# An LSTM ahead of a six-layer transformer: input projection kept in float32, its bf16 parts made later

## The reference, cut to what matters

```python
xW = jnp.einsum('ntd,dk->tnk', x, Wx) + b          # 1024 steps, 2 rows, 4*256 columns
def step(carry, xw_t):
    prev_h, prev_c = carry
    a = xw_t + prev_h @ Wh
    i, f, o = sigmoid(a[:, :H]), sigmoid(a[:, H:2*H]), sigmoid(a[:, 2*H:3*H])
    g = tanh(a[:, 3*H:])
    next_c = f * prev_c + i * g
    next_h = o * tanh(next_c)
    return ((next_h, next_c), next_h)
_, hs = jax.lax.scan(step, (h0, c0), xW)
# then, six times: attn_layer (windows of 64 keys) and ffn_layer, all in float32
```

## Time and profile before

| | |
|---|---|
| median of 3 runs | 5177.27 us (5176.47 to 5178.69) |
| profiled execution: span | 5175.6 us |
| profiled execution: own time | none is recorded; the median is 1.7 us above the span |
| busy over the span | PE 92%, PEld 72%, DVE 67%, ACT 50%, POOL 37% |
| LSTM stage (prologue and 136 steps) | until about 600 us |
| mean granted clock of PE | 0.934 of 2.4 GHz |

### The profile page before, as it was taken

How to read it: one execution, slowest core, us unless ns; L and a number is a source line. 1 busy time by engine, 2 the same in 40 slices (tenths; PEclk the granted TensorE clock), 3 DMA queues, 4 the chain that set the end, 5 groups by cost and what they waited for, 6 DMA issues and landing times.

```text
span 5175.6 us, 192189 instructions
## 1 busy us (share of the span) xinstructions
PE 4769.9 (92%) x79632; PEld 3728.4 (72%) x79632; DVE 3483.0 (67%) x14167; ACT 2608.7 (50%) x8192; POOL 1913.4 (37%) x2070
## 2 busy tenths in 40 slices
PE   4665699999999999999999999999999999999887
PEld 1445487777777787777777787777777787776666
DVE  8665577676676677677676677676676677676554
ACT  0112255555555555555555555555555555555654
POOL 3650233333333333333333333333333333334442
PEclk6555699999999999999999999999999999999999
DMA  3020122322322422322322422322322422323341
GB/s 131 2 88 0 38 83 81 117 86 88 114 83 80 124 82 81 117 85 87 113 84 81 123 82 81 116 86 84 117 84 80 122 83 81 117 85 106 109 130 48
DMA packets 311365, 463.54 MB, mean 90 GB/s; under 512 B 213264, under 2 KB 239888, under 8 KB 297616
## 3 DMA queue, kind: packets, MB, share of 16 engines
q1 hardware_dynamic: 310544, 451.92, 28.8%
HBM read 381.93 MB, written 69.93 MB: 87 GB/s over the span
## 4 chain that ended last, share of the span: by engine, by line
PE 63%; DVE 11%; issue 7%; POOL 4%; ACT 3%; POOLq 0%; DVEq 0%; ACTq 0%
PE mm L908 14%; PE gates L185 12%; PE st L1020 8%; PE gates L177 5%; PE dd L1020 4%; PE st L947 3%; PE pt L1047 3%; PE tt L920 3%; PE pt L1055 3%; PE pt L961 3%; DVE qk L1342 2%; POOL va L811 2%; DVE pr L1392 2%; PE dd L977 2%; PE st L989 1%
## 5 line engine op out<-in xcount | busy, mean ns | idle before, releaser
L796 POOL TENSOR_TENSOR turned<-raw,rotl 128x256 f32<-128x256 f32 x768 | 712.6, 943 | 1667.1 <-ACT raw L1139 1356.7
L908 PE MATMUL mm<-wqkv,xa 128*128 128x512 f32 x2304 | 1166.3, 618 | 12.3 <-DVE xa L1305 8.4
L185 PE MATMUL gates<-hp,whp 128*128 128x6 bf16 x28672 | 849.2, 165 | 22.1 <-DVE hp L230 22.1
L185 PEld LDWEIGHTS gates<-hp,whp 128*128 128x128 bf16 x28672 | 784.3, 96 | 56.8 <-DVE hp L230 29.4
L1190 ACT ACTIVATE pr<-st,nb,qn 128x128 f32<-128x128 f32 x1536 | 688.5, 464 | 36.7 <-DVE nb L1380 36.2
L192 ACT ACTIVATE state<-gsum 128x16 f32<-128x16 f32 x896 | 195.4, 218 | 1009.9 <-DVE gsum L200 1003.6
L908 PEld LDWEIGHTS mm<-wqkv,xa 128*128 128x128 f32 x2304 | 384.2, 193 | 241.6 <-issue 222.8
L200 DVE TENSOR_REDUCE gsum<-gates 128x16 f32<-128x48 f32 x896 | 183.1, 204 | 526.1 <-PE gates L185 526.1
L177 PEld LDWEIGHTS gates<-hp,whp 128*128 128x128 bf16 x14336 | 423.2, 96 | 141.5 <-issue 85.6
L177 PE MATMUL gates<-hp,whp 128*128 128x2 bf16 x14336 | 485.8, 163 | 26.2 <-DVE hp L215 26.2
L804 POOL TENSOR_TENSOR qn<-ss,power 128x8 f32<-128x8 f32 x192 | 320.6, 1670 | 496.7 <-DVE ss L1351 487.5
(11 more groups left out here) (135 smaller groups left out, 9778.8 us busy)
## 6 DMA issues: line engine op xcount, KB each, us to landing
wqkv<-in_Wqkv SPq DMA_DIRECT2D x288, 512.0 KB, 4.4
w<-in_W SPq DMA_DIRECT2D x48, 1364.0 KB, 6.1
wo<-in_Wo SPq DMA_DIRECT2D x48, 1024.0 KB, 4.9
w<-in_W SPq DMA_DIRECT2D x48, 768.0 KB, 4.5
kT<-k_windows SPq DMA_DIRECT2D x96, 256.0 KB, 5.4
va<-v_windows SPq DMA_DIRECT2D x96, 256.0 KB, 5.5
k_windows<-kT SPq DMA_DIRECT2D x96, 256.0 KB, 4.4
v_windows<-vb SPq DMA_DIRECT2D x96, 256.0 KB, 5.0
```

The lines of the kernel that those rows point to most:

```text
L185: last = nc.tensor.matmul(g[:, m * PARTS * BATCH:(m + 1) * PARTS * BATCH], self.whp[:, p, k, m * P:(m + 1) * P], self.hp[:, k, :, :].rearr ...
L796: ins = nc.gpsimd.tensor_tensor(dst[:, :, a, :], src[:, :, 1 - a, :], tab[:, :, a, :].broadcast_to([P, 8, HALF]), ALU.mult)
L908: ins = nc.tensor.matmul(mm[c % 2][:, :], shifted(xa, y.b, k), wqkv[:, c, k, :], start=(k == 1), stop=(k == 0))
```

## The change

The projection stays float32 in SBUF and DRAM (`XW32` = 16 numbers a token in place of 48 bf16). It is made in 8 blocks of 128 tokens, each of 4 pieces; a piece is two gate blocks, for both batch rows, in one PSUM bank: four float32 matmuls of 256 columns. Only the first block is made ahead of the steps. The other 28 pieces run one matmul behind each of the first 112 steps, and ACT evacuates them in two halves straight into `xw`, one behind the second and one behind the third step of the next piece. In this stage PE adds `xw` by a float32 matmul with the float32 identity, two of them per step (12 and 4 columns). POOL keeps only two memsets here; DVE splits `Wh` in seven instructions counting that for the bias. The loads are reordered: `Wh`, the first tokens of x, `Wx`, small ones, then the rest of x. SP writes each finished block to DRAM. In the layer stage SP loads float32 steps into `xw32`, and DVE splits them once per slot in four instructions (`split_steps`) into `xwp`, before `row_inv(x, 2)` of the slot ahead of their use.

```diff
+XW32 = GM * BATCH
-    def on_pe(self, nc, pe, t, g, go, ident16, xw_t):
+    def on_pe(self, nc, pe, t, g, go, ident, xw_t):
...
-            nc.tensor.matmul(g[:, oc:XWC], ident16[:, :], xw_t[:, oc:XWC], start=True, stop=False, skip_group_check=True)
-            nc.tensor.matmul(go[:, 0:oc], ident16[:, :], xw_t[:, 0:oc], start=True, stop=False, skip_group_check=True)
+        def first_part(bank, lo, hi):
+            return bank[:, lo:hi].rearrange("p (m q b) -> p m q b", q=PARTS, b=BATCH)[:, :, 0, :]
+        pe.wait_ge(self.out_summed, t + 1)
+        nc.tensor.matmul(first_part(g, oc, XWC), ident[:, :], pairs(xw_t[:, HC:XW32]), start=True, stop=False, skip_group_check=True)
+        nc.tensor.matmul(first_part(go, 0, oc), ident[:, :], pairs(xw_t[:, 0:HC]), start=True, stop=False, skip_group_check=True)
...
-        xw = sb("xw", [P, SEQ, XWC], BF16)
+        xw = sb("xw", [P, SEQ, XW32])
...
+        MP = 2
+        NB = SEQ // TILE
+        NE = GM // MP
+        NP = NB * NE
+        MATMULS = MP * KT
+        SPREAD = MATMULS * (NP - NE)
+        SPELL = SPREAD + MATMULS
...
-            for t in range(SPREAD):
+            for t in range(SPELL):
                 one_step(t, t % 2)
-                between(NE + t // STEPS_PER_PIECE, t % STEPS_PER_PIECE)
+                between(NE + t // MATMULS, t % MATMULS)
...
+            sp.dma_start(wh32[:, :, :], Wh).then_inc(wh_in, 16)
+            for k in range(KT):
+                sp.dma_start(by_batch(xT[:, :, :])[:, k, :, 0:TILE], by_batch(x_cols)[:, k, :, 0:TILE]).then_inc(xt_in, 16)
             sp.dma_start(wx_sb[:, :, :], Wx).then_inc(wx_in, 16)
-            sp.dma_start(xT[:, :, :], x_cols).then_inc(xt_in, 16)
...
+            for k in range(KT):
+                sp.dma_start(by_batch(xT[:, :, :])[:, k, :, TILE:SEQ], by_batch(x_cols)[:, k, :, TILE:SEQ]).then_inc(xt_rest, 16)
...
-            sp.wait_ge(xw_split, NE)
-            sp.wait_ge(late_split, len(LATE))
-            sp.dma_start(xw_dram[:, LEAD * XWC:SEQ * XWC], xw[:, LEAD:SEQ, :].rearrange("p t n -> p (t n)")).then_inc(spilled, 16)
+            for n in range(1, NB):
+                sp.wait_ge(xw_evac, MP * NE * (n + 1))
+                t0, t1 = max(LEAD, n * TILE), (n + 1) * TILE
+                sp.dma_start(xw_dram[:, t0 * XW32:t1 * XW32], xw[:, t0:t1, :].rearrange("p t n -> p (t n)")).then_inc(spilled, 16)
...
+            def piece(n, i):
+                if n >= NP:
+                    return
+                half, k = i // KT, i % KT
+                if n >= 2 and i == 0:
+                    pe.wait_ge(xw_evac, MP * (n - 1))
+                if n == NE and i == 0:
+                    pe.wait_ge(xt_rest, 16 * KT)
+                m = n % NE * MP + half
+                ins = nc.tensor.matmul(pj[n % 2][:, half * BATCH * TILE:(half + 1) * BATCH * TILE], wx_sb[:, k, m * P:(m + 1) * P],
+                                       by_batch(xT[:, :, :])[:, k, :, tokens(n)], start=(k == 0), stop=(k == KT - 1), skip_group_check=True)
...
+            def evacuate(n, half):
+                if half == 0:
+                    act.wait_ge(projected, n + 1)
+                m = n % NE * MP + half
+                dst = xw[:, tokens(n), m * BATCH:(m + 1) * BATCH].rearrange("p t b -> p b t")
+                src = pj[n % 2][:, half * BATCH * TILE:(half + 1) * BATCH * TILE].rearrange("p (b t) -> p b t", b=BATCH)
+                nc.scalar.activation(dst, src, ACT.Identity, bias=bias[:, m:m + 1], scale=1.0 if m // KT == 3 else 0.5).then_inc(xw_evac, 1)
+            def before(n, i):
+                if NE < n <= NP and i in (1, 2):
+                    evacuate(n - 1, i - 1)
...
+            dve.wait_ge(wh_in, 16)
+            wh_link(nc.vector.tensor_scalar(wh32[:, :, 0:3 * DIM], wh32[:, :, 0:3 * DIM], 0.25, None, ALU.mult))
+            wh_link(nc.vector.tensor_scalar(wh32[:, :, 3 * DIM:GATES], wh32[:, :, 3 * DIM:GATES], 0.5, None, ALU.mult))
+            wh_link(nc.vector.tensor_copy(whp[:, 0, :, :], wh32[:, :, :]))
+            wh_link(nc.vector.tensor_tensor(wh32[:, :, :], wh32[:, :, :], whp[:, 0, :, :], ALU.subtract))
             dve.wait_ge(h0_in, 32)
             nc.vector.tensor_scalar(bias[:, 0:3 * KT], bias[:, 0:3 * KT], 0.5, None, ALU.mult).then_inc(bias_ready, 1)
+            wh_link(nc.vector.tensor_copy(whp[:, 1, :, :], wh32[:, :, :]))
+            nc.vector.tensor_tensor(whp[:, 2, :, :], wh32[:, :, :], whp[:, 1, :, :], ALU.subtract).then_inc(wh_split, 1)
...
             def slot(x, y, steps, last, final, next_l, next_first):
                 if steps.n:
-                    sp.wait_ge(lstm.out_done, steps.first)
+                    if x.k:
+                        sp.wait_ge(xw_parts[0], x.it + 1)
+                    elif x.it:
+                        sp.wait_ge(xw_parts[1], x.it)
                     load_steps((x.k + 1) % 2, next_first)
...
-                            pe.wait_ge(xw_in[x.k], x.it * 16 + 16)
+                            pe.wait_ge(xw_parts[x.k], x.it + 1)
...
+            def split_steps(n, round_):
+                dve.wait_ge(xw_in[n], round_ * 16 + 16)
+                src, rest = xw32[:, n, :, :].rearrange("p t (m b) -> p t m b", b=BATCH), xw_rest[:, :, :].rearrange("p t (m b) -> p t m b", b=BATCH)
+                at = [xwp[:, n, :, :].rearrange("p t (m q b) -> p q t m b", q=PARTS, b=BATCH)[:, q] for q in range(PARTS)]
+                n_parts[0] += 1
+                first = 3 * (n_parts[0] - 1)
+                nc.vector.tensor_copy(at[0], src).then_inc(xw_chain, 1)
+                dve.wait_ge(xw_chain, first + 1)
+                nc.vector.tensor_tensor(rest, src, at[0], ALU.subtract).then_inc(xw_chain, 1)
+                dve.wait_ge(xw_chain, first + 2)
+                nc.vector.tensor_copy(at[1], rest).then_inc(xw_chain, 1)
+                dve.wait_ge(xw_chain, first + 3)
+                nc.vector.tensor_tensor(at[2], rest, at[1], ALU.subtract).then_inc(xw_parts[n], 1)
...
                 h_keep()
+                next_steps()
                 row_inv(x, 2)
```

More of the change, by code:

```diff
@@ L297, in lstm_stage @@
[L297 to L306, removed]
@@ L308, in parts_of @@
-        def parts_of(n):
-            m, b, t0 = PIECES[n]
-            return [xw[:, t0:t0 + 512, (m * PARTS + q) * BATCH + b] for q in range(PARTS)]
+        wh_chain, wh_split, h_chain0 = sem("wh_chain"), sem("wh_split"), sem("h_chain0")
+        projected, xw_evac = sem("projected"), sem("xw_evac")
+        MP = 2
[5 more added lines that the diff above has]
+        SPELL = SPREAD + MATMULS
+        assert SPELL <= LEAD and SPELL % 2 == 0 and (LEAD - SPELL) % UNROLL == 0
@@ L352, in _ @@
             nc.gpsimd.memset(zero, 0.0).then_inc(zeroed, 1)
[L353 to L381, removed]
@@ L383, in _ @@
         @block.tensor
         def _(pe):
-            pe.wait_ge(xt_in, 16)
+            pe.wait_ge(xt_in, 16 * KT)
             pe.wait_ge(wx_in, 16)
[L389 to L395, removed]
+            def piece(n, i):
[9 more added lines that the diff above has]
+                                       by_batch(xT[:, :, :])[:, k, :, tokens(n)], start=(k == 0), stop=(k == KT - 1), skip_group_check=True)
+                if i == MATMULS - 1:
@@ L396, in piece @@
                     ins.then_inc(projected, 1)
             for n in range(NE):
-                for k in range(KT):
-                    piece(n, k)
-            pe.wait_ge(xw_split, NE)
+                for i in range(MATMULS):
+                    piece(n, i)
+            pe.wait_ge(xw_evac, MP * NE)
             pe.wait_ge(wh_split, 1)
             pe.wait_ge(h_ready, 1)
-            steps(pe, lambda t, u: lstm.on_pe(nc, pe, t, ps[u], po[u], ident16, xw[:, t, :]), lambda n, phase: piece(n, phase) if phase < KT else None)
+            steps(pe, lambda t, u: lstm.on_pe(nc, pe, t, ps[u], po[u], ident, xw[:, t, :]), piece)
@@ L423, in _ @@
+            def before(n, i):
+                if NE < n <= NP and i in (1, 2):
+                    evacuate(n - 1, i - 1)
             for n in range(NE):
-                piece(n)
-            steps(act, lambda t, u: lstm.on_act(nc, act, t, True), lambda n, phase: piece(n) if phase == KT else None)
+                for half in range(MP):
+                    evacuate(n, half)
+            steps(act, lambda t, u: lstm.on_act(nc, act, t, True), before)
         @block.vector
         def _(dve):
-            n_chain = [0]
+            n_chain, n_wh = [0], [0]
@@ L445, in _ @@
             link(nc.vector.tensor_tensor(hp[:, :, 2, :], pairs(hrest[:, :]), hp[:, :, 1, :], ALU.subtract))
[L447 to L450, removed]
-                link(nc.vector.tensor_tensor(rest32, src, at[0], ALU.subtract))
-                link(nc.vector.tensor_copy(at[1], rest32))
-                nc.vector.tensor_tensor(at[2], rest32, at[1], ALU.subtract).then_inc(xw_split, 1)
-                dve.wait_ge(xw_split, n + 1)
             dve.wait_ge(zeroed, 2)
@@ L1309, in prologue, with next_steps @@
                 from_history(0, 1)
```

(6 more changed lines are left out.)

57 lines of the change are left out of this document (26 added, 31 removed).

## The result

The changed kernel took 5004.95 us (median of 4 runs, 5002.69 to 5007.01) against 5176.87 of the kernel before in the same session: ratio 0.9668, 95% interval 0.9656 to 0.968. The forecast was 5010 us. The profiled execution has a span of 5003.4 us, before 5175.6.

What follows compares the result with a forecast made beforehand. DVE's split bounded the prologue; DVE and ACT, projection matmuls or POOL casts bounded steps. 5175.6 - 114.7 - 56.6 + 4 = 5008.3 us, with the median 1.7 us above the span: 5010 us; 8-in-10 range 4982 to 5095.

Steps and rivals of the forecast that it cites:

- Prologue: Stretch before step 0: without the projection split, step 0 comes at 20.5 us instead of 135.2, saving 114.7 us.
- Steps: The 136 LSTM steps: 408.5 us instead of 465.1, saving 56.6 us (30 to 73).
- A step with projection: LSTM step with a float32 projection matmul behind it: 3.03 us instead of 3.23, bounds 2.88 and 3.27.
- The three exposed loads and two matmuls: Float32 xw adds on PE in a projection step: 0.66 us of exposed weight loads plus 0.1 for matmuls.
- Plain steps: The 24 LSTM steps without projection: 2.88 us each, set by DVE and ACT, not PE.
- Evacuation: ACT's two 256-element evacuations of a piece beside the steps: 0.4 to 0.7 us each, hidden in a gap.
- Layer stage: DVE's split in 84 slots, ahead of row_inv: 0.05 us a slot sticks out, 4 us lost (0 to 124).
- The clock's rise (1): TensorE's clock rises to 2.4 GHz in the steps: 17 us less, 4993 us; chance 0.13.
- Dearer identity loads (2): Float32 identity weight loads in the steps cost more: steps of 3.27 us, 27 us more, 5037 us; chance 0.12.
- The split sticking out (3): DVE's split in the layer slots sticks out 0.5 to 1.5 us a slot: 5050 to 5130 us; chance 0.18.
- Slower (4): Layer stage: full strided price plus POOL's pow holding the first cast, 3.1 us a slot, 5266 us; chance 0.02.
- The kernel does what it says (5): Opposite of a rival in which steps wait for projection of their own block; no cost seen; chance 0.01.

Runs made afterwards that it cites:

- e2: Kernel before without DVE's split of the first 16 projection pieces (ACT writes them as bf16, rests zero): 5095.49 us, ratio 0.9842.
- e4: Changed kernel with four blocks (512 tokens) projected ahead of step 0 and 16 pieces beside the steps: 5020.71 us, ratio 0.9699.
- e3: Changed kernel with the split of Wh back on POOL: 5015.04 us, ratio 0.9689.
- e1: Kernel before without POOL's split of the 16 later projection pieces (ACT writes them as bf16, rests zero): 5135.06 us, ratio 0.992.
- e5: Changed kernel plus 16 rounds of POOL casts and subtractions, on tiles nobody reads, beside the first 48 steps: 5092.19 us, ratio 0.9833.
- e7: Changed kernel with the out gate's float32 xw matmul replaced by a bf16 one on other data: 4995.83 us, ratio 0.9649.
- e6: Changed kernel with the split of each of the 84 slots made twice in the same place: 5115.52 us, ratio 0.9877.

## Why the prediction was right

*Prologue: 114.7 us forecast, 114.2 measured.* Wx came at 9.93 us (forecast 8.9), Wh at 5.87 (5.9). PE ended at 19.8, in the middle of its range, for two reasons: its first eight records ran at the pace of the lower clock and the other 24 at that of the higher, and piece 3 waited for ACT, whose table load of 1.28 us wasn't in my sum. I had picked 20.5 us from a range of 17 to 24 without forecasting either, so that it came within 0.5 us is in part luck. Wh's split took 8.7 us (8.1 to 11.6), hidden. The parts overlap, so experiments price them from different sides: DVE's split of the projection at least 79.7 us (e2), 128 instead of 512 tokens ahead 20.9 less 3.7 given back in the steps (e4), Wh on DVE 7.6 (e3).

*Steps: 56.6 forecast, 58.7 measured.* The split on POOL was the cause of the long steps: taken away it gives 60 us (e1), put back elsewhere it costs 87 (e5). A step with projection took 2.98 or 2.99 us, forecast 3.03. PE's work from sum of gates to L108 is 204.63 - 202.89 = 1.74 us, where the earlier trace rows have 138.50 - 136.51 = 1.99: 0.25 less, not 0.20. The three exposed loads and two matmuls that I put at 0.76 us run from 203.92 to 204.63, 0.71. Plain steps took 2.88 as forecast in the loop. The 1.16 us of idle time in the earlier trace rows stands ahead of L108, the first half, and not ahead of the second as the prediction says; that DVE and ACT set the plain step holds. The 7 odd intervals cost some 2 us. In six of them one DVE instruction (L159, L163, L164 or L167) starts 0.15 to 0.36 us late, in the seventh PE does. The six are steps 32, 42, 52, 62, 101 and 111, and the same ones in e7 at other times, so they are bound to a place in the code; the cause stays open.

*Evacuation: 0.4 to 0.7 us forecast, 0.67 measured, hidden.* It is at the upper end: half the elements of before take as long, now at a step of 64 bytes.

*Layer stage: 4 us forecast, 0.7 measured.* Casts took 0.25 us, not 0.34: they go at (0.253 - 0.17)/176 = 0.47 ns per element in spite of their 12-byte step. With them the split is 1.29 us against a cover of 1.49. It doesn't stick out, and the term should have been 0 (the prediction's 1.49 and 1.31 also count four gaps of 0.03 us where four instructions have three, which makes 1.45 and 1.28); 0.7 us is inside the spread. The rule in the Trainium skill, page "SBUF — State Buffer", section "Door 1: The DMA port swizzle", gave 0 and was nearer than my sum; the mean of 348 ns for the subtractions agrees with it as well.

*The rivals.* The clock's rise (1) didn't come: the granted clock fell to 0.50, that is 1.2 GHz, at 23.4 us, in the second step, and stayed there to the end of the steps, with PE busy 50.00 of 50 us at 300 us. The Trainium skill, page "TensorE: Matmul & The Clock Gate", section "What's actually happening", has sustained activity release the throttle; the pace of the prologue's matmuls, which doubled at 13.2 us, agrees with it, and the 404 us of steps, 97% busy by the records, don't. Had it risen, PE's work ahead of L108 could have given back 0.07 us a step by e7, since the floor is 2.92; what the rest of a step would gain wasn't measured. Dearer identity loads (2) didn't come: L101's and L102's loads fit into the 0.71 us. The split sticking out (3) is refuted for one split; e6 shows what stood behind it, 1.3 us a slot for the next. Slower (4) would have needed POOL's power to hold the DVE's split, which it doesn't; POOL's rotations hold a split in e6. The kernel does what it says (5): no step waits for its projection, and none of the 135 intervals is above 3.40 us.

No term was off by more than 4 us; measured minus forecast they are +0.5, -2.1 and -3.3 us, together the -4.9 from 5008.3 to the span of 5003.4.

## What to carry to other kernels

Work that is off the path by its dependencies can still be on it by its engine: four POOL instructions on data that nobody reads cost 5.4 us a round (e5), and POOL's split of a piece 3.8 us (e1), because DVE's smallest instructions stretch beside them. Before you give idle POOL time to a job, look for instructions of a few columns that take over 1 us in the trace, and price an engine's work from rows where it runs alone. And an idle stretch ahead of an engine's next wait is worth its length and no more: work of 1.29 us was free in 1.49, and the same work once more made each slot 1.3 us longer.

## What the runs showed of the hardware

- POOL and DVE slow each other down: POOL's cast of 128x512 takes 0.61 us alone (e3) and 1.53 beside DVE's split (the kernel before); DVE's 128x4 subtraction 0.16 alone and 1.4 to 1.8 beside a POOL subtraction or cast (e5). POOL's power of 128x8, 1.71 us long, stretched no DVE instruction of the split.
- The step of 12 bytes between bf16 pairs costs DVE nothing: a cast of 176 elements 0.25 us, a subtraction 0.34.
- ACT pays for the step of its writes: 0.68 us for 512 float32 elements in a row, 0.67 for 256 at 64 bytes (0.58 in the prologue, where two follow each other), 2.44 for 512 bf16 at 96 bytes (e2).
- An LSTM step without projection takes 2.92 us in unrolled code and 2.88 in the loop.
- In the changed kernel's prologue PE's first matmul records came 0.43 us apart, from 13.2 us on 0.21 us apart with a granted clock of 1.00 (2.4 GHz); from 23.4 us to the end of the steps the clock was 0.50 (1.2 GHz), with PE busy 97% by the records.
